# Flamingo block with cross-attention and an eight-expert FFN: first-layer weights loaded ahead of the slot reads, and the second early turn half a layer sooner

## The chip, the cores and the metric

The kernel runs on one core of one Trainium2 chip. The metric is device time in microseconds (us) of one execution, lower is better. The engines are PE (TensorE), DVE (VectorE), ACT (ScalarE), POOL (GpSimd) and SP (SyncE, which here only issues DMAs and waits).

## The reference

Four sequences of 512 tokens with 256 features. A 16-head cross-attention with mask and additive bias is followed by a feed-forward layer with 8 experts, of which each token uses the one with the highest gate value:

```python
x = x + tanh(g_xattn) * attention(layernorm(x), ctx, ctx, adj, mask)      # 4 x 512 x 256, 16 heads
h = layernorm(x).reshape(-1, 256)                                        # 2048 tokens
p = softmax(h @ gate_w.T); e = argmax(p)                                 # 8 experts
y = relu(h @ w1[e] + b1[e]) @ w2[e] + b2[e]                              # 256 -> 1024 -> 256
x = x + tanh(g_ffn) * (y * p[e])
```

## The kernel before, in words

**Attention.** A batch is one sequence. For each batch, 64 steps (`TILES`) each compute the scores of 128 queries against 512 keys for one head on PE (L931), take the row minimum and add the bias on DVE (L1551), shift on POOL (L672) or ACT (L1234), transpose on PE (L941), take the exponential on ACT (L1209), and every eighth step group is weighed with the values on PE (L953, `weigh`). Output projection, normalisation and routing of a batch are spread over the steps by tables (`USES`, `LAST_USES`). All engines run written-out programs and meet in semaphores only.

**Routing.** Each token gets a place in a table in DRAM, `slot_d`: routing goes in five rounds of four 128-token tiles, one round in each batch's steps and the last behind them, and for each tile POOL writes 128 entries of 8 bytes (token number and weight) by an indirect DMA (`to_slots`, L635). The table is later read back 128 entries at a time; such a group of 128 tokens of one expert is called a slot. There are 23 slots. The first five (`EARLY`) are full before the last round, whatever it brings, and are worked on beside the tail of the last batch; the other 18 (`LATE`) follow in a loop.

**One slot.** SP reads the slot's entries (`slots<-slot_d`) and the 1 MB first-layer weights of its expert (w1: 128 partitions of 8 KB). POOL gathers the 128 normalised rows from `xn_d` (L651 for the early ones, L732 later) and the 128 residual rows from `x1_d` (L658, L739). PE turns the rows (`early_turn`, L1019; `turn_rows`, L1095), ACT copies them to SBUF (`turned_rows`, L1272), PE computes the first layer in two halves of 16 matmuls (`early_hidden`, L1031; L1106), ACT applies the relu (`hidden`, L1278), PE computes the second layer (L1044; L1116), DVE adds bias and residual, and POOL scatters the rows to the output. The second-layer weights of all eight experts (w2, 1 MB each) stay in SBUF (`w2s`), which during attention holds the stacked queries and keys; the space of experts 4 and 6 is free after three quarters of the last batch's scores, that of 5 and 7 after all of them. No second layer starts before all eight have landed.

**SP's queue before,** from there on: w2 of experts 4 and 6 (after 48 of 64 score steps); w1 of early slot 0 when the early experts are known (`e_eid`); when the entries of the first four rounds have landed (`r_scat`), the five early slot reads; w1 of early slots 1 and 2; the attention output's rows to DRAM (`tail_pair`), and a wait until those have landed; w2 of experts 5 and 7; w1 of early slots 3 and 4. After the last routing: a wait for `r_eid` (experts of the late slots known) and `r_scat` (last entries written), the reads of late slots 0 and 1, their w1 loads, then a loop that reads each next slot and its weights when the buffers come free.

**POOL** waits for the five early slot reads (`early_index`) at step 59 of the last batch, in between two shifts that the attention steps need, then gathers the rows of early slot 0 and, three steps later, of early slot 1.

In the names of the trace, `w2s<-in_L_ffn_w` is a w2 load, and a load from `in_L_ffn_w` into `adjr`, `parts`, `xcin` or `pt` is a w1 load (their buffers are reused space). `parts<-xn_d,eidx` is the gather of an early slot's rows; `xT` from L1272 is the turned rows' copy, `adjm` the hidden layer's output.

Of the kernel before, what the change touches and what calls it, by code (L numbers as in the profile page):

```python
# [25 lines left out]
def build(nc, x, ctx_in, mask, g_xattn, g_ffn, adj, Wq, bq, Wk, bk, Wv, bv, Wo, bo,  # L26
          gate_w, w1, b1, w2, b2, out):
    B, S, E = x.shape
    X, _, DFF = w1.shape
    D = P // PAIRS  # L30
    H = E // D
# [21 lines left out]
    TILES = GROUPS * TPG  # L53
# [101 lines left out]
    with ExitStack() as st:  # L155
# [156 lines left out]
        def xg_bank(u):  # L312
            return bank[0][:, u * E:(u + 1) * E]

        def h_bank(u, c):
            return bank[1 + 2 * u + c // 4][:, (c % 4) * P:(c % 4 + 1) * P]
# [47 lines left out]
        def _(sp):  # L364
# [58 lines left out]
            def tail_pair(b, t, k, nxt):  # L423


                for u in range(2):
                    next_xres(b, nxt, k + u)
                for u in range(2):
                    rows_out(b, t, k + u)
                rows_free(b, k)  # L430
# [31 lines left out]
            def load_w2(e):  # L462
                sp.dma_start(w2s[:, e], w2[e].rearrange("(c p) f -> p c f", p=P)).then_inc(r_w2, 16)


            last = B - 1
# [9 lines left out]
            def early_w1(s):  # L476
                u = s % len(ew1)
                e = sp.value_load(eid[0:1, s:s + 1], min_val=0, max_val=X - 1)
                sp.dma_start(ew1[u], w1_v[ds(e, 1)].rearrange("x p k f -> p (x k) f")).then_inc(e_w1[u], 16)

            sp.wait_ge(s_stack, last * STACKED)
            sp.wait_ge(s_score, last * TILES + 6 * TILES // 8)
            for e in range(X // 2, X, 2):
                load_w2(e)
            sp.wait_ge(e_eid, 1)
            early_w1(0)
            sp.wait_ge(r_scat, B * (16 * QT))
            for s in range(EARLY):
                at = sp.value_load(base_i[0:1, s:s + 1], min_val=0, max_val=X * TOK)
                sp.dma_start(slots[:, s], slot_d[ds(at, P), :]).then_inc(e_slots, 16)  # L490
            sp.wait_ge(s_xT, B * 4)
            for s in range(1, 3):
                early_w1(s)
            tail_pair(last, last * QT, 2, last * QT + 2)
            sp.wait_ge(s_score, B * TILES)
            for e in range(X // 2 + 1, X, 2):
# [9 lines left out]
            def load_slots(j, v, after=None):  # L506


                at = sp.value_load(base_i[0:1, ds(j + EARLY, 1)], min_val=0, max_val=X * TOK)
                if after is not None:  # L510
                    sp.wait_ge(f_xt, after + EARLY)
                sp.dma_start(slots[:, ds(j + EARLY, 1), :].rearrange("p s a -> p (s a)"),
                             slot_d[ds(at, P), :]).then_inc(r_slots[v], 16)

            def load_w1(j, v, after=None):

                e = sp.value_load(eid[0:1, ds(j + EARLY, 1)], min_val=0, max_val=X - 1)
                if after is not None:
                    sp.wait_ge(f_h, FC * (after + EARLY))
                sp.dma_start(w1s[:, v], w1_v[ds(e, 1)].rearrange("x p k f -> p (x k) f")).then_inc(f_w1[v], 16)  # L520

            sp.wait_ge(r_eid, 1)
            sp.wait_ge(r_scat, (B + 1) * (16 * QT))
            for v in range(2):
                load_slots(v, v)
            for v in range(2):
                load_w1(v, v)
            with sp.Fori(0, LATE // 2 - 1) as i:
                for v in range(2):
                    load_slots(i * 2 + (v + 2), v, i * 2 + v + 1)  # L530
# [257 lines left out]
        def _(pe):  # L788
# [227 lines left out]
            def early_turn(s):  # L1016
                pe.wait_ge(e_row[s % EROWS], 16 * (s // EROWS + 1))
                for k in range(EC):
                    mm = pe.transpose(xg_bank(s % 2)[:, k * P:(k + 1) * P],  # L1019
                                      erow[s % EROWS][1][:, k * P:(k + 1) * P], ident[:])  # L1020
                mm.then_inc(f_xt, 1)

            def early_hidden(s, half):
                u = s % 2
                w = s % len(ew1)
                if half == 0:
                    pe.wait_ge(e_w1[w], 16 * (s // len(ew1) + 1))
                    pe.wait_ge(f_xgT, s + 1)
                for c in range(half * FC // 2, (half + 1) * FC // 2):
                    for k in range(EC):  # L1030
                        mm = pe.matmul(h_bank(u, c), ew1[w][:, k, c * P:(c + 1) * P], xgT[:, u, k],  # L1031
                                       start=k == 0, stop=k == EC - 1)
                    mm.then_inc(f_h, 1)
# [14 lines left out]
            def last_tail(what, k=0):  # L1048
                i = next(i for i, (n, w, a) in enumerate(TAIL_A) if w == what and (what == "gate" or a == k))
                tail_use(B, i + LAST_SHIFT, what, TAIL_A[i][2])  # L1050
# [9 lines left out]
            pe.wait_ge(s_osb, B * GROUPS + 2)  # L1060
            last_tail("heads", 0)
            last_tail("heads", 1)
            early_hidden(0, 1)
            early_turn(1)
            last_tail("turn", 0)
            last_tail("turn", 1)
            early_hidden(1, 0)
# [64 lines left out]
        def _(act):  # L1132
# [137 lines left out]
            def turned_rows(s, u):  # L1270
                act.wait_ge(f_xt, s + 1)
                act.activation(xgT[:, u], xg_bank(u).rearrange("p (k q) -> p k q", k=EC),  # L1272
                               ACT.Copy).then_inc(f_xgT, 1)

            def hidden(s, u, e, half):
                act.wait_ge(f_h, s * FC + (half + 1) * (FC // 2))
                for c in range(half * FC // 2, (half + 1) * FC // 2):
                    act.activation(hT[:, u, c], h_bank(u, c), ACT.Relu, bias=b1c[:, ds(e * FC + c, 1)]  # L1278
                                   ).then_inc(f_hT, 1)

            def expert_of(s):
                return act.value_load(eid[0:1, ds(s, 1)], min_val=0, max_val=X - 1)

            def last_tail(what, k):
                i = next(i for i, (n, w, a) in enumerate(TAIL_A) if w == what and a == k)
                tail_use(B, i + LAST_SHIFT, what, k)
# [7 lines left out]
            act.wait_ge(e_eid, 1)  # L1294
            e = expert_of(0)
            hidden(0, 0, e, 0)
            hidden(0, 0, e, 1)
            turned_rows(1, 1)
            last_tail("turn", 0)
            last_tail("turn", 1)  # L1300
            e = expert_of(1)
# [5 lines left out]
            e = expert_of(2)  # L1307
# [4 lines left out]
            for s in range(3, EARLY):  # L1312
                e = expert_of(s)
# [451 lines left out]
```

## Time and profile before

| | |
|---|---|
| time, median of 3 runs | 571.88 us (569.12 to 575.5) |
| the profiled execution's own time | 572.78 us |
| its span, first to last instruction | 570.8 us |
| PE busy | 532.1 us, 93% of the span |
| DVE, ACT, POOL busy | 298.7, 304.6, 304.2 us |
| mean granted TensorE clock | 0.996 |
| the chain that ended last | PE 51%, DMA 18%, issue 10%, DVE 7%, POOL 5% |

The profiled execution took 2.0 us more than its span, which is start and end outside the instructions. Times inside the trace are counted from the span's start. The attention ends at about 378 us and the late loop begins at about 431 us; the change touches what lies between 349 and 432 us. The profiled execution lies 0.9 us above the median of the three timed runs.

### The profile page before, as it was taken

What the parts mean: (1) busy time and instruction counts of PE and PEld (TensorE: products, weight loads), DVE (VectorE), ACT (ScalarE), POOL (GpSimd) and SP (SyncE); (2) the same over time, 40 slices, a digit from 0 to 9 for tenths busy, and PEclk for the clock granted to TensorE, in tenths of its full rate; (3) what the DMA queues carried; (4) which work ended last, traced back from release to release, by engine and by line L of the source; (5) the groups of instructions that cost most, each with busy time, mean ns of one, the idle gap of its engine ahead of it and who ended that gap; (6) DMA issues with size and microseconds to landing.
All of it is one profiled execution on the core that took longest, in us unless ns stands there. A gap on an engine that the chain in (4) does not pass through costs nothing.

```text
span 570.8 us, 13582 instructions
## 1 busy us (share of the span) xinstructions
PE 532.1 (93%) x4126; PEld 405.8 (71%) x4127; DVE 298.7 (52%) x908; ACT 304.6 (53%) x675; POOL 304.2 (53%) x461
## 2 busy tenths in 40 slices
PE   7999999989999989999999998879997899999996
PEld 5576666657566657666666765548897899999995
DVE  2676677875577876576876878813510111111111
ACT  4466676666677566678665676443232233333331
POOL 6345476765466665467573646451425445544441
PEclk9999999999999999999999999989999999999999
DMA  8633526301216410105510078778137656555650
GB/s 280 206 107 101 170 87 201 103 20 48 101 39 201 131 41 1 76 18 167 177 49 1 28 247 213 161 258 313 57 37 279 195 166 163 189 196 192 198 186 6
DMA packets 51392, 77.22 MB, mean 135 GB/s; under 512 B 9945, under 2 KB 34601, under 8 KB 51209
## 3 DMA queue, kind: packets, MB, share of 16 engines
q1 hardware_dynamic: 46600, 67.72, 37.2%
q0 software_dynamic: 4096, 8.29, 5.2%
q8 instruction: 29, 0.48, 0.4%
q10 hardware_dynamic: 640, 0.52, 0.3%
q14 instruction: 27, 0.21, 0.2%
HBM read 52.76 MB, written 7.89 MB: 106 GB/s over the span
## 4 chain that ended last, share of the span: by engine, by line
PE 51%; DMA 18%; issue 10%; DVE 7%; POOL 5%; ACT 4%; SPq 4%; POOLq 1%; DVEq 0%; ACTq 0%
PE bank L941 13%; DMA out_y<-cT,sidx 10%; PE bank L953 9%; PE bank L931 7%; PE bank L834 4%; DVE prob L1551 3%; DMA slot_d<-pair,posi 3%; SPq L345 3%; PE bank L1116 2%; PE bank L869 2%; PE bank L915 2%; PE bank L1031 2%; PE bank L1106 2%; ACT pt L1209 2%; POOL rows L739 2%
## 5 line engine op out<-in xcount | busy, mean ns | idle before, releaser
L1551 DVE CUSTOM_DVE_ANT_0 prob<-bank,adjm 128x512 f32<-128x512 f32 x256 | 172.5, 687 | 82.1 <-issue 50.1
L672 POOL TENSOR_SCALAR prob<-prob,negmax 128x512 f32<-128x512 f32 x192 | 133.2, 698 | 130.6 <-DVE negmax L1551 125.7
L1209 ACT ACTIVATE pt<-bank 128x512 f32<-128x512 f32 x256 | 150.3, 594 | 87.6 <-PE bank L941 83.3
L941 PE MATMUL bank<-ident,prob 128*128 128x128 f32 x1024 | 154.8, 274 | 4.6 <-POOL prob L672 2.3
L941 PEld LDWEIGHTS bank<-ident,prob 128*128 128x128 f32 x1024 | 124.2, 141 | 43.5 <-issue 14.7
L1278 ACT ACTIVATE adjm<-bank,colsm 128x128 f32<-128x128 f32 x184 | 52.6, 368 | 107.5 <-PE bank L1106 86.0
L931 PE MATMUL bank<-w2s 128*128 128x512 bf16 x256 | 97.5, 381 | 7.6 <-DVE negmax L1551 4.9
L953 PE MATMUL bank<-pt,vals 128*32 128x256 f32 x1024 | 69.1, 389 | 0.7 <-DVE vals L1365 0.5
L1727 DVE TENSOR_TENSOR cT<-bank,maski 128x256 f32<-128x256 f32 x18 | 7.6, 424 | 117.3 <-PE bank L1116 103.3
L1106 PEld LDWEIGHTS bank<-xT,pt 128*128 128x128 f32 x576 | 67.1, 192 | 1.8 <-ACT xT L1272 1.0
L1106 PE MATMUL bank<-xT,pt 128*128 128x128 f32 x576 | 67.3, 275 | 0.7 <-ACT xT L1272 0.7
L1116 PE MATMUL bank<-w2s,adjm 128*128 x288 | 65.4, 380 | 0.0
L1234 ACT ACTIVATE prob<-prob,negmax 128x512 f32<-128x512 f32 x64 | 45.9, 717 | 31.5 <-DVE negmax L1551 31.2
L1116 PEld LDWEIGHTS bank<-w2s,adjm 128*128 128x128 f32 x288 | 53.3, 190 | 6.5
L931 PEld LDWEIGHTS bank<-w2s 128*128 128x128 bf16 x256 | 25.7, 100 | 29.9 <-DVE negmax L1551 14.6
L953 PEld LDWEIGHTS bank<-pt,vals 128*32 128x32 f32 x1024 | 27.0, 109 | 23.0 <-issue 10.2
L635 POOL DMA_INDIRECT slot_d<-pair,posi x20 | 21.0, 1049 | 12.0 <-DVE posi L1474 5.1
L748 POOL DMA_INDIRECT out_y<-cT,sidx x18 | 18.1, 1007 | 15.0 <-DVE cT L1732 10.1
L732 POOL DMA_INDIRECT rows<-xn_d,gidx x18 | 18.0, 998 | 14.3 <-POOL gidx L730 14.3
L739 POOL DMA_INDIRECT rows<-x_d,xidx x18 | 17.4, 969 | 14.2 <-POOL xidx L737 14.2
L601 POOL TENSOR_TENSOR adjm<-adjr,maski 128x512 f32<-128x512 f32 x16 | 20.6, 1285 | 2.6 <-ACT maski L1198 2.4
L1551 DVE DVE_READ_ACCUMULATOR2_ANT negmax<- 128x1 f32 x256 | 20.9, 82 | 0.0
(192 smaller groups left out, 604.0 us busy)
## 6 DMA issues: line engine op xcount, KB each, us to landing
pt<-in_L_ffn_w SPq DMA_DIRECT2D x19, 1024.0 KB, 5.2
w2s<-parts SPq DMA_DIRECT2D x96, 128.0 KB
w2s<-in_L_ffn_w SPq DMA_DIRECT2D x8, 1024.0 KB, 9.9
maski<-in_mask_Bx1xSxS_ik SPq DMA_DIRECT2D x4, 1024.0 KB, 5.4
w2s<-parts SPq DMA_DIRECT2D x56, 64.0 KB, 2.1
xres<-in_x SPq DMA_DIRECT2D x18, 128.0 KB, 2.2
x_d<-rows SPq DMA_DIRECT2D x18, 128.0 KB, 1.7
xn_d<-rows SPq DMA_DIRECT2D x18, 128.0 KB, 2.5
```

The source lines that it names most:

```text
L672: po.tensor_scalar(prob[:, m], prob[:, m], -1.0, negmax[:, m:m + 1], ALU.mult, ALU.add).then_inc(s_shpool, 1)
L739: po.indirect_dma_start(rows[:, v, 0:E], None, x1_d, bass.IndirectOffsetOnAxis(ap=xidx[:, v:v + 1], axis=0)).then_inc(f_x1[v], 16)
L834: mm = pe.matmul(o[:], wT[:, w, k, m * P:(m + 1) * P], src[:, k], start=k == 0, stop=k == EC - 1)
L931: pe.matmul(sc_bank[m][:], q, k, start=True, stop=True).then_inc(s_score, 1)
L941: mm = pe.transpose(tr_bank[n % NTB][:, c * P:(c + 1) * P], prob[:, n % TILES % NB, c * P:(c + 1) * P], ident[:])
L953: mm = pe.matmul(pv_bank[32 * j:32 * j + 32, (g % 2) * HALF:(g % 2 + 1) * HALF], vals[:, c, hg * HG + j, :], pt[:, g % 2, c, j, :], start= ...
L1106: mm = pe.matmul(h_bank(u, c), w1s[:, v, k, c * P:(c + 1) * P], xgT[:, u, k], start=k == 0, stop=k == EC - 1)
L1116: mm = pe.matmul(y_bank(u), hT[:, u, c], w2s[:, ds(e, 1), c, :].rearrange("p x e -> p (x e)"), start=c == 0, stop=c == FC - 1)
L1209: act.activation(pt[:, g % 2, :, j, q2 * P:(q2 + 1) * P], tr_bank[c % NTB][:].rearrange("p (c q) -> p c q", c=QT), ACT.Exp).then_inc(s_cac ...
L1234: act.activation(prob[:, m], prob[:, m], ACT.Identity, scale=-1.0, bias=negmax[:, m:m + 1]).then_inc(s_shact, 1)
L1278: act.activation(hT[:, u, c], h_bank(u, c), ACT.Relu, bias=b1c[:, ds(e * FC + c, 1)]).then_inc(f_hT, 1)
L1551: ve.tensor_tensor_reduce(out=prob[:, m % NB], in0=sc_bank[m % NS][:], in1=adjm[:, qt], scale=-1.0, scalar=BIG, op0=ALU.add, op1=ALU.min, ...
```

## The change

Four edits. In the last batch SP issues w1 of early slots 0, 1 and 2 first, then reads the five slots, and only then loads w2 of experts 4 and 6. After the last routing, w1 of late slots 0 and 1 is loaded when the experts are known, before the wait for the table's last entries and before the two slot reads. On PE, `early_turn(1)` moves ahead of the second half of early slot 0's first layer, and on ACT `turned_rows(1, 1)` with it. Nothing is added or removed: each engine has as many instructions as before.

```diff
             sp.wait_ge(s_stack, last * STACKED)
-            sp.wait_ge(s_score, last * TILES + 6 * TILES // 8)
-            for e in range(X // 2, X, 2):
-                load_w2(e)
             sp.wait_ge(e_eid, 1)
-            early_w1(0)
+            sp.wait_ge(s_xT, B * 4)
+            for s in range(3):
+                early_w1(s)
             sp.wait_ge(r_scat, B * (16 * QT))
             for s in range(EARLY):
                 at = sp.value_load(base_i[0:1, s:s + 1], min_val=0, max_val=X * TOK)
                 sp.dma_start(slots[:, s], slot_d[ds(at, P), :]).then_inc(e_slots, 16)
-            sp.wait_ge(s_xT, B * 4)
-            for s in range(1, 3):
-                early_w1(s)
+            sp.wait_ge(s_score, last * TILES + 6 * TILES // 8)
+            for e in range(X // 2, X, 2):
+                load_w2(e)
             tail_pair(last, last * QT, 2, last * QT + 2)
...
             sp.wait_ge(r_eid, 1)
+            for v in range(2):
+                load_w1(v, v)
             sp.wait_ge(r_scat, (B + 1) * (16 * QT))
             for v in range(2):
                 load_slots(v, v)
-            for v in range(2):
-                load_w1(v, v)
...
+            early_turn(1)
             early_hidden(0, 1)
-            early_turn(1)
             last_tail("turn", 0)
...
             hidden(0, 0, e, 0)
+            turned_rows(1, 1)
             hidden(0, 0, e, 1)
-            turned_rows(1, 1)
```

SP in the last quarter of the last batch, before (L463 loads w2, L479 loads w1, L490 reads a slot; in brackets the semaphores that it waits for):

```order
L463 DMA w2s<-in_L_ffn_w 128x8x256 [waits score,stack]
L463 DMA w2s<-in_L_ffn_w 128x8x256
L478 TENSOR_LOAD eid [waits e_eid]
L478 ISA x2
L479 ISA
L479 DMA adjr<-in_L_ffn_w 128x2x1024
L489 TENSOR_LOAD base_i [waits r_scat]
L489 ISA x2
L490 ISA
L490 DMA slots<-slot_d 128x2
```

The same place now begins with three w1 loads; the five slot reads follow them.

```order
L478 TENSOR_LOAD eid [waits xT,e_eid,stack]
L478 ISA x2
L479 ISA
L479 DMA adjr<-in_L_ffn_w 128x2x1024
L478 TENSOR_LOAD eid
L478 ISA x2
L479 ISA
L479 DMA parts<-in_L_ffn_w 128x2x1024
```

Behind the last of the five slot reads SP now has the w2 pair, ahead of `tail_pair`:

```order
L489 DMA slots<-slot_d 128x2
L463 DMA w2s<-in_L_ffn_w 128x8x256 [waits score]
L463 DMA w2s<-in_L_ffn_w 128x8x256
L402 DMA xres<-in_x 128x256 [waits t_x1] x2
L407 DMA x_d<-rows 128x256 [waits t_row]
L408 DMA xn_d<-rows 128x256
```

The w2 loads have moved from the head of this stretch to behind the reads, and two w1 loads from behind the reads to ahead of them.

SP after the last routing, before (L512 reads a slot, L520 loads w1):

```order
L509 TENSOR_LOAD base_i [waits t_out0,t_x2T,t_out1,r_scat,r_eid]
L509 ISA x2
L512 ISA
L512 DMA slots<-slot_d 128x2
L509 TENSOR_LOAD base_i
```

And now, from the second of the two w1 loads (L519) to the first slot read; the wait for `r_eid` alone stands before the first of them:

```order
L516 TENSOR_LOAD eid
L516 ISA x2
L519 ISA
L519 DMA pt<-in_L_ffn_w 128x2x1024
L508 TENSOR_LOAD base_i [waits r_scat]
L508 ISA x2
L511 ISA
L511 DMA slots<-slot_d 128x2
```

The wait for `r_scat` stands behind the two w1 loads now.

ACT around early slot 0's hidden layer, before: the copy of early slot 1's turned rows (L1272) follows both halves (L1278).

```order
L1278 ISA
L1278 ACTIVATE adjm<-bank,colsm 128x128
L1272 ACTIVATE xT<-bank 128x2x128 [waits f_xt]
L1181 ACTIVATE atT<-bank 128x256 [waits m]
L1181 ACTIVATE atT<-bank 128x256 [waits t_atT,m]
```

Now it stands between the two halves:

```order
L1277 ISA
L1277 ACTIVATE adjm<-bank,colsm 128x128
L1271 ACTIVATE xT<-bank 128x2x128 [waits f_xt]
L1277 ISA [waits f_h]
L1277 ACTIVATE adjm<-bank,colsm 128x128
```

One copy has moved ahead of four relu instructions; PE's turn of the same rows has moved ahead of 16 matmuls in the same way.

## Rows read from the trace of the kernel before

**Rows 1.** Chain of waits, 320 to 381 us (start, length, what).

```profile
...
354.31 10.65 DMA slot_d<-pair,posi
...
370.19 1.70 DMA slots<-slot_d
...
373.12 7.55 DMA parts<-xn_d,eidx
...
```

**Rows 2.** Timeline of SP's DMA issues, 345 to 376 us.

```profile
...
349.57 1.12 SPq L463 DMA_DIRECT2D w2s<-in_L_ffn_w  x2
359.32 0.39 SPq L479 DMA_DIRECT2D adjr<-in_L_ffn_w  x1
365.70 4.84 SPq L490 DMA_DIRECT2D slots<-slot_d  x5
371.31 0.40 SPq L479 DMA_DIRECT2D parts<-in_L_ffn_w  x1
372.46 0.40 SPq L479 DMA_DIRECT2D xcin<-in_L_ffn_w  x1
...
```

**Rows 3.** Timeline of POOL, 370 to 380 us (in brackets: idle before, releaser).

```profile
...
372.05 0.19 POOL L645 COPY eidx<-slots 128x5 int32<-128x5 int32 x1 [1.78 <-DMA slots<-slot_d]
...
374.27 1.36 POOL L672 TENSOR_SCALAR prob<-prob,negmax 128x512 f32<-128x512 f32 x2
...
```

**Rows 4.** Timeline of PE, 373.5 to 392 us.

```profile
...
373.76 1.07 PE L953 MATMUL bank<-pt,vals 128*32 128x256 f32 x16
...
377.58 0.66 PE L941 MATMUL bank<-ident,prob 128*128 128x128 f32 x4 [0.50 <-POOL prob L672]
380.80 0.41 PE L1019 MATMUL bank<-ident,parts 128*128 128x128 f32 x2 [2.56 <-DMA parts<-xn_d,eidx]
381.14 2.75 PE L953 MATMUL bank<-pt,vals 128*32 128x256 f32 x32
383.81 2.86 PE L1031 MATMUL bank<-xT,adjr 128*128 128x128 f32 x16
...
391.02 2.02 PE L1031 MATMUL bank<-xT,parts 128*128 128x128 f32 x16 [1.04 <-ACT xT L1272]
...
```

**Rows 5.** Timeline of ACT, the last exponential of attention.

```profile
...
378.27 0.60 ACT L1209 ACTIVATE pt<-bank 128x512 f32<-128x512 f32 x1 [0.37 <-PE bank L941]
...
```

**Rows 6.** Busy us per engine in stretches, PEclk, DMA share (us), GB/s.

```profile
...
364.00:366.00 2.00, 1.68 (x12) 1.00 (x10) 1.97 (x5) 1.72 (x5) 1.18 (x3) 1.00 0.65 66
382.00:384.00 2.00, 2.00 (x21) 0.74 (x14) 0.00 (x0) 0.07 (x1) 0.43 (x1) 0.53 0.70 242
384.00:386.00 2.00, 2.00 (x12) 2.00 (x13) 0.00 (x0) 0.32 (x1) 0.00 (x0) 0.62 0.22 65
388.00:390.00 2.00, 1.99 (x18) 1.75 (x17) 0.68 (x2) 0.53 (x3) 0.00 (x0) 1.00 1.05 359
416.00:422.00 6.00, 6.00 (x41) 5.59 (x41) 1.16 (x3) 2.33 (x9) 0.00 (x0) 1.00 0.48 26
428.00:431.00 3.00, 0.23 (x3) 0.20 (x2) 0.91 (x2) 0.00 (x0) 2.21 (x4) 1.00 1.04 386
...
```

**Rows 7.** Gathers issued 373 to 376 us: count, median us to landing.

```profile
...
parts<-xn_d,eidx POOLq DMA_INDIRECT x2, 7.5
```

**Rows 8.** The same, issued 398 to 401 us.

```profile
...
parts<-xn_d,eidx POOLq DMA_INDIRECT x2, 3.7
```

**Rows 9.** Chain of waits, 380 to 570 us.

```profile
...
413.37 8.71 DMA slot_d<-pair,posi
...
```

**Rows 10.** Timeline of all engines, 413 to 433 us.

```profile
...
414.57 0.28 DVE L1718 TENSOR_SCALAR base_i<-bf,least 128x19 int32<-128x19 f32 x1
...
424.80 0.18 POOL L730 COPY gidx<-slots 128x1 int32<-128x1 int32 x1 [9.16 <-DMA slots<-slot_d]
...
425.81 0.99 POOL L732 DMA_INDIRECT rows<-xn_d,gidx  x1 [0.83 <-POOL gidx L730]
...
430.79 0.41 PE L1095 MATMUL bank<-ident,rows 128*128 128x128 f32 x2 [2.77 <-DMA rows<-xn_d,gidx]
...
```

## The prediction

> **What bounds the kernel now.** I read the chain of waits first, then the timelines of the engines around the places that the diff touches, then the DMA views there. PE is busy 93% of the span, but the chain leaves PE between 354 and 381 us. There it runs through the last table write of POOL, which needs 10.65 us to land, the five slot reads (1.70 us for the last), and the gather of early slot 0's rows, 7.55 us [rows 1]. PE meanwhile works off the attention and then stands for 2.56 us until the rows are there [rows 4]. A second, smaller stop is the 1.04 us before early slot 1's first layer: PE waits for ACT's copy of the turned rows, which queues behind slot 0's relus [rows 4]. The third place is the start of the late loop, where PE stands 2.77 us for gathered rows [rows 10]. The reader should see in each case which step lands last, because the change moves only steps of SP's queue and one turn.
>
> **The w2 pair leaves the table writes' time.** The two w2 loads are issued from 349.57 us, w1 of slot 0 at 359.32, and the table writes are in flight until 354.31 + 10.65 = 364.96 [rows 1, 2]. At the end of the kernel the same four writes run with next to nothing beside them (26 GB/s in all) and the last needs 8.71 us from its issue [rows 6, 9]. So without the pair the wait for `r_scat` should end 1.9 us sooner, at 363.0, as the near bound. The early writes are issued at wider distances, so that less is queued when the last one goes out; I take 360 to 361 us, an estimate, and keep 363 to 365 as the bad end.
>
> **Three w1 loads go ahead of the reads.** SP spends 1.15 us per w1 load (371.31 to 372.46) [rows 2]. Starting at 359.32 it is through with three at 362.8. The five reads are issued over 4.84 us [rows 2], the last at 367.4, and it lands 1.70 us later [rows 1] or when the 3 MB ahead of it are through. At the 359 GB/s of a stretch full of weight loads [rows 6] these 3.15 MB take 8.8 us, from 360 to about 368.8. So the table is read at 369 to 369.5, against 371.9 before. POOL, which stood 1.78 us for it [rows 3], no longer waits, and its shifts from 374.27 on come up to 1.78 us sooner. PE's last transposes follow such a shift after a wait of 0.50 us [rows 4], but PE has the 16 matmuls from 373.76 to 374.83 ahead of them; I count 0.9 us. That puts PE's end of the attention at 377.3 in place of 378.24.
>
> **The w2 pair comes behind the reads.** It is issued at about 367.9 and moves from 369. Behind it stand two loads and four stores of `tail_pair`, 0.79 MB, then POOL's gather, now issued at about 371.3. The pair and the rows are 2.9 MB, 8.0 us at 359 GB/s, so until 377; the gather lands at about 378. **Here I chose against an even share:** the gather issued at 373.12 with 2 MB of w1 just ahead took 7.5 us, the same gather later 3.7 [rows 2, 7, 8]. It behaved as if it queued behind what was issued first. The Trainium skill ("DMA: Bandwidth & Descriptors", Queues, rings and completion order) says that each DMA engine goes round its queues packet by packet, so a gather on POOL's queue would not wait out SP's loads, and the gain here would be the 3.1 us worked out below. In this trace the gather's 7.5 us speaks against it.
>
> **What PE gets of it.** Turn at 378.0, then the weighing at about 378.5; it began at 381.14 before [rows 4]. Its own inputs are no bar: the last exponential ends at 378.87 [rows 5], less the 0.9 us that moves with the shifts. That is **2.6 us**. Were the gather there at 377.3 the weighing would begin at 378.0, and the gain be 3.1; should the writes still land at 363 to 365, the reads, the pair and the gather all move back two to three us, and no more than 0.5 to 1 us is left.
>
> **The clock.** After the stop of 2.56 us the granted clock is 0.53 and 0.62 in the next two stretches of 2 us [rows 6], which is 1.2 GHz for most of them. 32 weighing matmuls take 2.75 us there, where 16 took 1.07, and 16 of the first layer take 2.86, where 2.02 is usual [rows 4]: (2.75 - 2.14) + (2.86 - 2.02) = 1.45 us. With a stop of 0.7 us instead I expect the clock to stay at 2.4 GHz, **1.5 us**; zero is the other end, since in the stop of 2.77 us at 428 us [rows 10] the granted clock stayed at 1.00 [rows 6], so the link is not a firm one.
>
> **The turn sooner.** PE's turn of slot 1 stands ahead of 16 matmuls, and ACT copies its rows ahead of four relus. The rows are needed at about 383.5 then, after the weighing and half a first layer; their gather goes out some 3 us behind slot 0's, near 374, and has 9 us. PE goes from the attention's turns straight into slot 1's first layer: the 1.04 us of [rows 4] goes, and ACT's later copies for the output projection are covered by these 16 matmuls (2.02 us). **1.0 us.**
>
> **The w2 pair of experts 5 and 7, and the second layer.** That pair waits for `tail_pair` to land, which is not later than before, since less is queued ahead of it. The first second layer is far behind; I put this at nothing. If it were late, PE would wait for it whole.
>
> **The late loop's start.** The experts are known at 414.85 us [rows 10], so the two w1 loads go out at about 415.5 and 416.7, while the table writes are in flight until 413.37 + 8.71 = 422.08 [rows 9]. That gives and takes. The gather issued at 425.81 has landed by 430.7, 4.9 us later [rows 10], with a w1 load issued just ahead of it; without one it should take 3.7 us [rows 8], which gives up to 1.1. But while table writes are in flight other transfers crawl: 66 GB/s in a stretch before 366 with w1 of slot 0 outstanding, 26 GB/s at 416 to 422 with a gather outstanding [rows 6]. At 66 GB/s only 0.4 MB of the 2.1 MB are through by 422, and the rest needs 4.7 us at 359 GB/s, to 426.8. The slot reads stand behind it in SP's queue; the first had landed by 424.80 before [rows 10], and would now land 2.0 us later: 1.0 us lost. At full rate the pair would be through in time and the 1.1 stay whole. I take a loss of **0.7 us**, near the slow end, because both rows with table writes in flight are slow ones. What the loads do to the writes themselves is a rival.
>
> **The sum.** 2.6 + 1.5 + 1.0 - 0.7 = 4.4 us. The profiled execution's 572.78 us would be 568.4, and the median of 571.88 becomes **567.5 us**, 0.8% less. About 1% is what a measurement of this kernel can tell from no change.
>
> **Rivals.**
> (a) Everything comes out at its good end: the gather is not held by the w2 pair, and the late w1 pair is through before the reads: 3.1 + 1.5 + 1.0 + 1.1 = 6.7, so 565.2 us. For it: DMA is all but idle at 416 to 422, and the gathers of [rows 8] needed 3.7 us only. Against it: the 7.5 us of [rows 7], and the 66 GB/s. Chance 0.27. The skill's rule on the queues, above, would make the first part of it true.
> (b) The early table writes do not land sooner, because three w1 loads press on them in place of two w2 loads. Then the chain through table, reads and gather keeps its length: 0.8 + 0 + 1.0 - 0.7 = 1.1, so 570.8 us. For it: 10.65 us against 8.71 with and without loads, so loads do press. Against it: the w1 loads start 5 us after the last write is issued. Chance 0.2.
> (c) Slower than before: the two late w1 loads lengthen the last table writes, on which the late slot reads, and PE behind them, wait. If the writes wait out the pair as the gather of 7.5 us waited out 2 MB, they land 2.1 MB / 359 GB/s = 5.8 us later; the reads then have nothing ahead of them and the gather gives its 1.1. With the early part as in (b), 0.8 + 1.0 - 5.8 + 1.1 = -2.9, so 574.8 us. It decides once the writes land later by more than the early gains and 1.1 us: by 6.2 us if the early gains come whole, by 2.9 if they are those of (b). For it: 10.65 us with loads beside against 8.71 without. Against it: that is 1.9 us, not 5.8. Chance 0.06.
> (d) The change does not do what it says: the stop before the first turn stays because something else is last, such as the row gather behind `tail_pair`'s stores. That is the time of (b), and is in its chance.
>
> **How the numbers follow.** Forecast 0.47, (a) 0.27, (b) and (d) 0.2, (c) 0.06. Faster by over 1% means under 566.2 us: (a), and a little of the forecast's spread, 0.31. Slower by over 1% is over 577.6, beyond (c) as worked out; 0.04 is for the spread of the runs around it (569.12 to 575.5 before). The rest is 0.65. The range goes from 564.4, a little below (a), to 571.4, just beyond (b).
>
> **What would show it.** In the changed kernel's timelines: w2 of experts 4 and 6 issued at 367 to 369; no idle time of POOL before L645; the first early turn with at most 1 us of idle before it, at 377 to 379; no clock under 1.00 at 380 to 386; no wait for ACT before slot 1's first layer. In the late part, seen from the last table write's issue, its landing after 9 to 11 us and PE's first late turn after about 18 us, where it was 17.4. I am wrong if the table writes before 365 still take over 10 us from the last issue, if the gather still takes over 7 us and PE's stop stays, or if the last writes take 12 us and more.

## The result, and the profile after

The changed kernel needs 575.39 us (median of 20 runs, 572.03 to 578.27), the kernel before 571.92 (20 runs, 568.31 to 578.33). The ratio is 1.0063, 95% interval 1.0038 to 1.0087: 3.6 us slower, 2.2 to 5.0, where 4.4 us faster was forecast. The profiled execution after took 573.35 us (span 571.5, mean granted clock 0.989), the one before 572.78. Its own time hides most of the loss, so the places have to be read one by one.

SP's queue after, the place of [rows 2]:

```profile
...
359.40 0.39 SPq L479 DMA_DIRECT2D adjr<-in_L_ffn_w  x1
360.59 0.38 SPq L479 DMA_DIRECT2D parts<-in_L_ffn_w  x1
361.73 0.38 SPq L479 DMA_DIRECT2D xcin<-in_L_ffn_w  x1
362.89 4.85 SPq L489 DMA_DIRECT2D slots<-slot_d  x5
367.78 1.06 SPq L463 DMA_DIRECT2D w2s<-in_L_ffn_w  x2
...
380.33 1.01 SPq L463 DMA_DIRECT2D w2s<-in_L_ffn_w  x2
...
412.05 1.15 SPq L519 DMA_DIRECT2D pt<-in_L_ffn_w  x2
...
```

POOL and PE after, from the index copy to early slot 1's first layer, the places of [rows 3, 4]:

```profile
...
371.38 0.19 POOL L644 COPY eidx<-slots 128x5 int32<-128x5 int32 x1 [1.07 <-DMA slots<-slot_d]
...
```

```profile
...
378.81 0.41 PE L1018 MATMUL bank<-ident,parts 128*128 128x128 f32 x2 [1.12 <-DMA parts<-xn_d,eidx]
379.15 1.93 PE L952 MATMUL bank<-pt,vals 128*32 128x256 f32 x32
381.02 2.05 PE L1030 MATMUL bank<-xT,adjr 128*128 128x128 f32 x16
...
386.57 1.95 PE L1030 MATMUL bank<-xT,parts 128*128 128x128 f32 x16
...
```

The edits did what they say. PE's stop before the first early turn is 1.12 us in place of 2.56, the weighing begins at 379.15 in place of 381.14 and takes 1.93 us in place of 2.75, and the wait for ACT's copy is gone (386.57 has none). So far the profile is nearly the one that was forecast: the stop was to be at most 1 us, the weighing to begin 2.6 us sooner (it is 2.0), and POOL, which was no longer to wait for the slot reads, still stands 1.07 us for them. The chain of waits shows the other half, beside [rows 1, 9]:

```profile
...
367.39 3.83 DMA slots<-slot_d
...
372.44 5.91 DMA parts<-xn_d,eidx
...
408.84 9.59 DMA slot_d<-pair,posi
...
419.16 6.79 DMA slots<-slot_d
...
```

The last table write goes out at 408.84, 4.5 us sooner than 413.37. But the slot reads, issued when it has landed, need 6.79 us. In the kernel before, the chain has 1.72 us for them:

```profile
...
422.92 1.72 DMA slots<-slot_d
...
```

Timelines of POOL and PE after, beside [rows 10]:

```profile
...
426.11 0.18 POOL L729 COPY gidx<-slots 128x1 int32<-128x1 int32 x1 [14.99 <-DMA slots<-slot_d]
427.12 0.99 POOL L731 DMA_INDIRECT rows<-xn_d,gidx  x1 [0.83 <-POOL gidx L729]
...
```

```profile
...
409.06 3.73 PE L1030 MATMUL bank<-xT,pt 128*128 128x128 f32 x32
...
430.08 0.66 PE L1094 MATMUL bank<-ident,rows 128*128 128x128 f32 x2 [6.38 <-DMA rows<-xn_d,gidx]
431.29 6.28 PE L1105 MATMUL bank<-xT,pt 128*128 128x128 f32 x32 [0.54 <-ACT xT L1271]
437.41 0.38 PE L1094 MATMUL bank<-ident,rows 128*128 128x128 f32 x2
...
```

PE stands for 6.38 us where it stood for 2.77, and its first late layer takes 6.28 us where 32 such matmuls took 3.73 at 409.06. The stretches after tell both (busy us of each engine, granted clock, DMA share, GB/s; beside [rows 6]):

```profile
...
360.00:362.00 2.00, 1.69 (x11) 1.45 (x12) 1.72 (x8) 1.25 (x3) 1.18 (x2) 1.00 0.62 80
362.00:364.00 2.00, 2.00 (x26) 1.18 (x24) 1.82 (x6) 0.88 (x2) 0.20 (x1) 1.00 1.02 406
364.00:366.00 2.00, 1.71 (x12) 1.03 (x10) 1.96 (x5) 1.72 (x5) 1.15 (x3) 1.00 1.03 422
380.00:382.00 2.00, 2.00 (x30) 1.38 (x21) 0.00 (x0) 0.00 (x0) 1.45 (x2) 1.00 0.52 123
...
412.00:414.00 2.00, 2.00 (x15) 1.71 (x14) 0.00 (x0) 1.65 (x7) 0.00 (x0) 1.00 0.77 27
414.00:416.00 2.00, 2.00 (x11) 1.77 (x10) 0.00 (x0) 0.80 (x4) 0.00 (x0) 1.00 0.66 64
416.00:418.00 2.00, 2.00 (x18) 1.92 (x17) 0.91 (x2) 0.00 (x0) 0.00 (x0) 1.00 1.04 63
418.00:420.00 2.00, 2.00 (x21) 2.00 (x20) 0.00 (x0) 1.14 (x4) 0.00 (x0) 1.00 0.61 162
420.00:422.00 2.00, 2.00 (x12) 1.79 (x11) 0.00 (x0) 1.14 (x4) 0.00 (x0) 1.00 1.05 420
422.00:424.00 2.00, 1.71 (x8) 1.15 (x7) 0.15 (x1) 0.00 (x0) 0.00 (x0) 1.00 0.92 359
424.00:426.00 2.00, 0.00 (x0) 0.00 (x0) 0.76 (x2) 0.00 (x0) 0.00 (x0) 1.00 0.09 17
426.00:428.00 2.00, 0.00 (x0) 0.00 (x0) 0.00 (x0) 0.00 (x0) 1.06 (x2) 0.55 0.00 0
432.00:434.00 2.00, 2.00 (x11) 2.00 (x11) 0.00 (x0) 0.00 (x0) 1.19 (x3) 0.50 0.28 68
...
```

The granted clock is 1.00 behind the early stop (380 to 382) and 0.50, the lower level, behind the late one. The two w1 loads were issued from 412.05. While the table writes are in flight, to 418.43, the DMA engines show shares of 0.77, 0.66 and 1.04 and still move only 27 to 64 GB/s: 0.31 MB in six us. Then come 162, 420 and 359 GB/s, 1.88 MB, and at 424 the traffic is over. The read lands 1.95 us after that.

### The profile page after: what moved, and what is told of

Read it like the earlier page. It is cut to its first block, busy times and chain, and to the rows that moved or that the text cites. A ratio compares the mean times of both kernels' runs of the same rounds, so it can differ in the third digit from the quotient of the medians.

```text
span 571.5 us, 13581 instructions
## 1 busy us (share of the span) xinstructions
PE 532.6 (93%) x4126; PEld 407.1 (71%) x4127; DVE 298.9 (52%) x908; ACT 304.6 (53%) x675; POOL 304.0 (53%) x461
## 4 chain that ended last, share of the span: by engine, by line
PE 47%; DMA 18%; issue 11%; DVE 8%; POOL 5%; SPq 4%; ACT 4%; POOLq 1%; another core or an unknown queue 1%; DVEq 0%; ACTq 0%
PE bank L940 13%; DMA out_y<-cT,sidx 10%; PE bank L952 9%; PE bank L930 7%; DVE prob L1550 4%; PE bank L833 4%; SPq L345 3%; PE bank L868 2%; PE bank L914 2%; ACT pt L1208 2%; DMA slots<-slot_d 2%; PE bank L1115 2%; POOL rows L738 2%; DMA slot_d<-pair,posi 2%; PE bank L1030 2%
## 5 line engine op out<-in xcount | busy, mean ns | idle before, releaser
L1105 PEld LDWEIGHTS bank<-xT,pt 128*128 128x128 f32 x576 | 69.5, 198 | 1.8 <-ACT xT L1271 0.9
L1105 PE MATMUL bank<-xT,pt 128*128 128x128 f32 x576 | 69.8, 281 | 0.5 <-ACT xT L1271 0.5
L738 POOL DMA_INDIRECT rows<-x_d,xidx x18 | 17.4, 969 | 14.2 <-POOL xidx L736 13.4
```

The source lines that it names most:

```text
L738: po.indirect_dma_start(rows[:, v, 0:E], None, x1_d, bass.IndirectOffsetOnAxis(ap=xidx[:, v:v + 1], axis=0)).then_inc(f_x1[v], 16)
L1105: mm = pe.matmul(h_bank(u, c), w1s[:, v, k, c * P:(c + 1) * P], xgT[:, u, k], start=k == 0, stop=k == EC - 1)
```

## The experiments

Each ratio is to the kernel before, measured beside it. "Late pair ahead" is the edit behind the last routing; "early edits" are the other three. What was read from each profiled execution stands together here, in us. The fourth column is from the issue of the last table write to its landing, the fifth from that issue to the first late turn, the sixth the rest of the span from that issue. The last says behind which of PE's two stops (before the first early turn, before the first late turn) the granted clock fell to 0.50.

| kernel | first early turn | last table write issued | it lands after | late turn after | rest of span | half clock behind the stops |
|---|---|---|---|---|---|---|
| before | 380.80 | 413.37 | 8.71 | 17.42 | 157.4 | early |
| before_2 | 380.30 | 412.68 | 9.97 | 18.86 | 158.1 | both |
| before_3 | 380.74 | 413.31 | 9.11 | 18.06 | 157.4 | both |
| before_busy | 382.19 | 413.19 | 10.14 | 18.94 | 158.2 | none |
| turn_only | 380.90 | 412.89 | 9.10 | 17.94 | 160.4 | both |
| sp_early_only | 379.90 | 412.42 | 8.95 | 19.00 | 161.9 | both |
| early_only | 379.26 | 409.35 | 9.86 | 18.76 | 158.1 | late |
| early_only_2 | 381.77 | 411.45 | 9.59 | 18.35 | 159.4 | late |
| x_later | 380.31 | 410.00 | 8.97 | 17.72 | 161.4 | late |
| late_busy | 379.95 | 411.26 | 9.52 | 18.27 | 157.8 | early |
| busy_both | 380.13 | 409.84 | 9.47 | 18.30 | 161.0 | none |
| late_only | 381.36 | 413.91 | 9.96 | 21.93 | 164.8 | both |
| after | 378.81 | 408.84 | 9.59 | 21.24 | 162.7 | late |
| after_2 | 380.64 | 410.31 | 10.08 | 22.01 | 164.5 | late |
| pool_reads | 380.53 | 410.29 | 10.43 | 22.00 | 163.9 | late |
| after_busy | 380.79 | 412.10 | 10.55 | 22.40 | 164.1 | both |
| one_w1 | 381.97 | 413.20 | 9.46 | 18.85 | 163.2 | both |

**early_only**: all edits but the late one. The late part is as before:

```diff
             sp.wait_ge(r_eid, 1)
-            for v in range(2):
-                load_w1(v, v)
             sp.wait_ge(r_scat, (B + 1) * (16 * QT))
             for v in range(2):
                 load_slots(v, v)
+            for v in range(2):
+                load_w1(v, v)
```

> All edits but the late one: after the last routing SP again waits for the table's last entries, reads late slots 0 and 1, and then loads their w1. Theory Q (the loss is made in the late part: the slot reads stand behind 2 MB of w1 in SP's queue, and PE's longer stop brings the slow clock): the early part gains what the trace of the changed kernel shows at its last routing, 4.5 us, so about 567.5 us, ratio to before 0.990 to 0.994. Theory W (the w1 loads lengthen the last table writes, and that is the whole loss): the same 567.5, last write 8.7 us from its issue to landing. Theory E (the early part itself loses in most executions and the one trace is not typical): 573 us or more.

Measured: 0.9981, interval 0.9951 to 1.0011 (572.96 us). Its chain of waits:

```profile
...
372.88 6.17 DMA parts<-xn_d,eidx
...
409.35 9.86 DMA slot_d<-pair,posi
...
420.04 1.73 DMA slots<-slot_d
...
422.94 4.83 DMA rows<-xn_d,gidx
...
```

The read is back at 1.73 us. So the loss is in the late edit, and the early ones gain 1.1 us or nothing that can be told. The first two theories expected about 567.5 us here, the 4.5 us of the one trace of after; that did not come.

**late_only**: the kernel before with the late edit alone.

```diff
             sp.wait_ge(r_eid, 1)
+            for v in range(2):
+                load_w1(v, v)
             sp.wait_ge(r_scat, (B + 1) * (16 * QT))
             for v in range(2):
                 load_slots(v, v)
-            for v in range(2):
-                load_w1(v, v)
```

> Only the late edit: w1 of late slots 0 and 1 ahead of the wait for the table's last entries and of the two slot reads. Theory Q: the reads land about 6.8 us after their issue where it was 1.7, PE's first late turn begins 21 us after the last table write's issue (17.4 before), and the clock is slow for part of the next 10 us: 4 to 8 us slower than before, 576 to 580. Theory W: the last write needs 12 us and more, the reads still 1.7. Theory E: no difference from before.

Measured: 1.0083, 1.005 to 1.0117 (579.69 us), 4.7 us slower. The two halves add up to the whole: 0.9981 and 1.0083 against 1.0063. Its chain:

```profile
...
413.91 9.96 DMA slot_d<-pair,posi
...
424.60 7.11 DMA slots<-slot_d
...
```

The write lands after 9.96 us, within the 8.71 to 10.14 of the kernels without the late edit; the read takes 7.11. It is mainly the reads that wait, not the writes.

**after_busy**: the changed kernel with PE's late stop filled, by the kernel's own `keep_busy` (matmuls of ones that nothing reads).

```diff
             pe.wait_ge(r_w2, 16 * X)
+            keep_busy(55, bank[7])
             turn_rows(0, 0)
```

> The changed kernel with 55 matmuls of ones into a free bank between the last early second layer and the first late turn, some 6 us of PE work while it would stand; they compute nothing that is used. Theory Q with the clock as part of it: no slow clock between 420 and 440 us, 3 us or more faster than the changed kernel, 571 to 573 us. If the clock has no part in the loss: the same as the changed kernel, 575.

Measured: 1.0068, 1.0038 to 1.0098 (578.72 us). PE's idle time before the late turn falls to 1.48 us, the turn comes no sooner (22.40 us after the write's issue), and the half clock is still there, shorter: under 1.00 at 434 to 440, where in after it was from 426 to 438. Shortening it gains nothing that can be told (1.0068 against 1.0063); since the clock did fall, the run does not show what none of it would give. Two things say that it is not the cause: the late turn is late before the slow stretch costs anything, and before_2 and before_3 have the half clock behind the late stop too and end 158.1 and 157.4 us after the last table write's issue, where before ends after 157.4 without it.

**pool_reads**: the changed kernel, in which POOL issues the first two late slot reads on its own queue.

```diff
             for v in range(2):
                 load_w1(v, v)
-            sp.wait_ge(r_scat, (B + 1) * (16 * QT))
-            for v in range(2):
-                load_slots(v, v)
...
+            for v in range(2):
+                at = po.value_load(base_i[0:1, v + EARLY:v + EARLY + 1], min_val=0, max_val=X * TOK)
+                po.dma_start(slots[:, v + EARLY], slot_d[ds(at, P), :]).then_inc(r_first[v], 16)
```

> The changed kernel, with the reads of late slots 0 and 1 issued by POOL on its own queue (after the same waits) in place of SP. Theory Q in the form that only SP's own queue holds the reads back: they land within 3 us of their issue although the w1 pair is still loading, PE's first late turn begins 18 us after the last table write's issue, and the time is 568 to 571. If the DMA engines work off all queues in the order of issue: the reads land after 5 to 7 us as in the changed kernel, and the time is 575.

Measured: 1.0073, 1.0042 to 1.0105 (577.98 us). The chain's row of the read, and the stretches from there:

```profile
...
422.57 5.63 DMA slots<-slot_d
...
```

```profile
...
422.00:424.00 2.00, 2.00 (x11) 1.74 (x10) 0.00 (x0) 1.03 (x4) 0.85 (x2) 1.00 1.02 414
424.00:426.00 2.00, 1.21 (x6) 0.73 (x4) 0.61 (x2) 0.00 (x0) 0.30 (x1) 1.00 1.00 391
426.00:428.00 2.00, 0.00 (x0) 0.00 (x0) 0.30 (x1) 0.00 (x0) 0.00 (x0) 0.90 0.24 93
...
```

Another queue gives no way past: the read takes 5.63 us, and lands 2 us after full traffic ended at about 426.2. POOL issues it 1.85 us behind the landing of the writes, SP did after 0.73, and so it lands 17.9 us after the last write's issue, as in after_2. POOL's own gather ahead of it, issued at 411.57, had landed 9.3 us later, before the read went out, so it did not hold the read. That SP's own queue orders the read behind the loads falls as the cause; the bytes issued first were served first, or nearly so, across the queues. No run has a read on POOL's queue with nothing ahead, so what this queue adds of itself is not known.

**one_w1**: only the first late w1 load ahead of the reads.

```diff
-            for v in range(2):
-                load_w1(v, v)
+            load_w1(0, 0)
             sp.wait_ge(r_scat, (B + 1) * (16 * QT))
             for v in range(2):
                 load_slots(v, v)
+            load_w1(1, 1)
```

> The changed kernel with one late w1 load ahead of the wait for the table and of the reads, the second behind them. Theory Q (reads stand behind the bytes issued before them): some 0.3 MB pass while the table is written, 0.7 MB are left, so the reads land 3.5 to 4.5 us after their issue (6.8 with two loads, 1.7 with none), and the time lies about half way between the changed kernel and the kernel with the early edits alone: 2 us under the changed one. Theory W (the loads lengthen the table writes, whatever their number): no better than the changed kernel.

Measured: 1.0037, 1.001 to 1.0063 (574.78 us). Half the bytes ahead, about half the length:

```profile
...
413.20 9.46 DMA slot_d<-pair,posi
...
423.72 4.16 DMA slots<-slot_d
...
```

1.73, 4.16 and 6.8 to 7.1 us with none, one and two loads of 1 MB ahead: 2.4 to 2.9 us for each, about what 1.05 MB take at 359 to 420 GB/s. But in this trace the first late turn comes 18.85 us after the write's issue, within the 17.4 to 19.0 of the kernels with no load ahead: the gather behind the read, with no load just ahead of it, takes back what the read lost. The time is 2.1 us longer all the same, and the trace has 4.2 us of PE's waits for gathered rows after 440 us, where the others have 0 to 3.1. So the dose shows the read's length, and not that the whole of the time follows from it.

**turn_only** and **sp_early_only** halve the early edits: the second early turn (on PE and ACT) alone, and SP's new order up to `tail_pair` alone.

```diff
+            early_turn(1)
             early_hidden(0, 1)
-            early_turn(1)
```

> Of the changed kernel only the early turn of slot 1 and its copy half a layer sooner. PE's wait of 1.0 us before slot 1's first layer is gone; the last table write is issued 1.0 us sooner. 1.0 us faster if the late part hands it on; the same if the table writes or the clock take it back.

> Of the changed kernel only SP's early order (three w1 loads, slot reads, then w2 of experts 4 and 6); the turn and the late order as before. By the first traces (last routing 1.3 to 4.5 us sooner with the early order and the turn together) I expect the last table write of POOL issued 1 to 3 us sooner than before, and 1 to 3 us of time, if the late part gives nothing back; no gain if it does.

Measured: 0.998, 0.9947 to 1.0013, and 0.9996, 0.9969 to 1.0023. In turn_only PE no longer waits for the turned rows' copy. In sp_early_only the first early turn comes 0.4 to 0.9 us sooner than in the three traces of before. Their sum is about that of early_only; neither can be told from nothing.

**x_later**: early_only with the gather that follows the last table writes on POOL (the residual rows of early slot 4) moved behind the first two late gathers.

```diff
             for t in range(QT):
                 to_slots(t)
-            early_x(EROWS + 1)
...
             for v in range(2):
                 gather_normed(v, 0, v)
+            early_x(EROWS + 1)
```

> The kernel with the early edits alone, and POOL's gather of early slot 4's residual rows moved from right behind the last table writes to behind the two gathers of late rows. It asks what holds the table writes up, which need 8.7 to 9.9 us from the last issue with no load beside them but this gather. If the gather presses on them: 7 to 8 us, and up to 2 us less time than with the early edits alone. If they are slow by themselves: unchanged, and the later gather may cost some tenths of a us because an early output waits for it.

Measured: 0.9983, 0.995 to 1.0016 (570.6 us). The writes land after 8.97 us, in the lower part of what is seen with the gather; no effect on the time can be told from early_only's.

**busy_both**, **before_busy** and **late_busy** fill PE's stops: the early edits with both filled, the kernel before with both filled, the early edits with the late one filled.

```diff
             pe.wait_ge(e_eid, 1)
+            keep_busy(12, bank[2])
             early_turn(0)
...
             pe.wait_ge(r_w2, 16 * X)
+            keep_busy(30, bank[7])
             turn_rows(0, 0)
```

> The kernel with the early edits alone, and matmuls of ones into free banks where PE stands: 12 (1.3 us) before the first early turn, 30 (3.2 us) before the first late turn; they compute nothing that is used. The traces so far have a stretch of slow clock behind one or both stops in every execution. If the clock is what takes the early gain back: no or less slow clock behind both, and 2 to 4 us less than before (ratio 0.993 to 0.997), 1 to 3 us less than with the early edits alone. If the clock falls all the same or is not the cause: as with the early edits alone, 0.998, or some tenths of a us more.

> The kernel before with 12 matmuls of ones ahead of the first early turn and 30 ahead of the first late turn, whose results nothing reads; no load is moved. If what made the kernel with the early edits and these matmuls 0.5% faster is only the clock, this one gains the same, 0.995 to 0.997, with the granted clock at 1.00 behind both stops; if it needs the earlier table writes as well (last one issued near 409.5 us in place of 413), this one lies at 0.998 to 1.000 and its last table write is issued at 412 or later.

> The early edits alone, with the 30 matmuls ahead of the first late turn and none at the early stop. If the slow clock at the late stop is what gives back the two to three us by which the early edits bring the last table write forward, this lies where the kernel with both fillings was, 0.994 to 0.997; if the late filling does nothing, it lies where the early edits alone were, 0.998, with later pauses of the loop taking what the clock gives.

Measured: 0.9954 (0.9923 to 0.9985, 571.72 us), 0.9968 (0.9938 to 0.9999, 573.48 us, its before 575.33) and 0.9965 (0.9934 to 0.9997, 571.48 us, the same before). Stretches of before_busy behind both stops, beside [rows 6]:

```profile
...
382.00:384.00 2.00, 1.81 (x30) 1.12 (x34) 0.00 (x0) 0.38 (x1) 1.70 (x2) 1.00 1.09 403
384.00:386.00 2.00, 2.00 (x26) 1.59 (x17) 0.00 (x0) 0.39 (x1) 0.06 (x1) 1.00 0.41 137
432.00:434.00 2.00, 1.23 (x9) 1.00 (x10) 0.00 (x0) 0.38 (x1) 1.21 (x3) 1.00 1.01 412
434.00:436.00 2.00, 2.00 (x21) 2.00 (x20) 0.00 (x0) 0.61 (x3) 1.39 (x3) 1.00 0.65 189
...
```

The clock holds at 1.00 behind both. All three are faster than before, busy_both by 0.46%, and that version beats both kernels. The filling alone gives 0.3%, the early edits alone 0.2% (not told from nothing), both 0.5%: the figures add, but the intervals overlap and do not tell the three apart.

**before_2**, **before_3**, **early_only_2** and **after_2** are one more profiled execution each of kernels that ran already.

> The kernel before once more, one look, since one trace of it stands for 20 runs that spread over 10 us. In its first trace the clock was slow behind the early stop (382 us) and not behind the late one. If that was typical: the same again, late turn 17.4 us after the last table write's issue and 140 us from there to the end. If it was a lucky execution: slow clock at the late stop too, and 142 to 143 us to the end.

> The kernel before a third time, the same question: is a slow clock behind the late stop, and how long are the steps from the last table write to the late turn (17.4) and from there to the end (140.0).

> The kernel with the early edits alone a second time, one look. Last table write's issue at 409.4 us if no slow clock follows the early stop, near 412 if one does; late turn 18 to 19 us later.

> The changed kernel once more, for a second trace. If the late loop's start is the cause, the first slot read again lands 6.5 to 7.2 us after its issue, and the first late turn comes 21 to 22.5 us after the last table write's issue; if the profiled execution was an odd one, these are nearer to the 1.7 and 18 us of the kernel before.

Their times were 572.66, 572.64, 572.72 and 576.67 us. after_2 repeats the read's length:

```profile
...
421.12 7.07 DMA slots<-slot_d
...
```

They show what one trace cannot: the half clock is behind the early stop in all traces with before's SP order and no filling there (five of five), and behind the late stop in two of before's three. The 1.00 of [rows 6] at 428 to 431, behind a stop of 2.77 us, was one execution's.

## Why the prediction was wrong

**The failed step is the late loop's start.** The term was a loss of 0.7 us; late_only gives 4.7 (2.9 to 6.7), and so does the changed kernel's ratio against early_only's. In the traces the first late turn comes 21.2 to 22.4 us after the last table write's issue with two w1 loads ahead (mean of five 21.9), and 17.4 to 19.0 without (mean of eleven 18.3): 3.6 us, where 0.7 was forecast. (The working gave 2.0 - 1.1 = 0.9; it was written as 1.0 and taken as 0.7, "near the slow end", without a row.) Step by step, counted from that issue in the changed kernel's trace:
- The pair was to be through after 13.4 us (426.8 against 413.37). It was through after some 15.2 (424 against 408.84). The loads went out 3.2 us after the write's issue, not 2.1. The crawl was in the sum, at 0.4 MB; it moved 0.3 MB, the write landed 0.9 us later, and the full rate came up only about a us behind the landing (162 GB/s at 418 to 420).
- The read was taken to land together with the pair. Its own 1.7 us (the last early read of [rows 1]) come on top: it landed 1.95 us after the traffic ended, 17.1 us after the write's issue, not 13.4. This is a little over half of the 3.7 us, and it needed no new price: the row was there, and I counted a transfer behind a load as one that ends with the load.
- The gather gained more than the 1.1 us of the forecast: PE turns 2.96 us after it is issued at 427.12, where it was 4.98 [rows 10]. That gives back 0.9 of the 3.7.

So the mechanism (reads queued behind w1, w1 crawling beside the writes) was right, but for the words "in SP's queue", which pool_reads takes out; the size at the turn was wrong by a factor of five. What is left of the 4.7 us, about 1 us, lies behind the late turn, where the rest of the span differs by more than the turn does; it isn't traced to one place.

**The w2 pair out of the writes' time: right in the writes, wrong in what follows.** The early entries had landed by 360.1 in the changed kernel, 359.7 to 363.5 in all traces with the new SP order, against 363.6 to 366.5 with the old one: the 360 to 361 of the estimate is the better end of that (means 361.6 and 365.1). But the reads landed at 371.2, where 369 to 369.5 was forecast. The w1 loads issued from 359.40 moved 80 GB/s until 362 and 406 to 422 after, so that 3.1 MB ended at about 369.5, and the read's own time came on top, again left out. That is the same mistake as in the late part, at the first place where I made it. In the other traces it is worse: POOL's gather of slot 0's rows went out at 373.4 in the mean of the eleven, at 372.9 in the five with the old order and no filling. The 3.5 us gained at the writes are gone by then.

**What PE gets of it: 2.6 us forecast, 0.5 measured.** The first early turn stands at 380.4 in the mean of the eleven traces with SP's new order, and at 380.8 in the five with the old one and no filling. In the trace of after the weighing began 2.0 us sooner; that trace is the best of the eleven, and the others are up to 3.2 us behind it. The 0.5 us are left of the gather, which went out 0.5 us later in the mean but took 6.8 us in place of 7.8. The stop, forecast at 0.7 us, went from 2.6 to 1.8 in the mean of the traces without filling.

**The gather behind the w2 pair** landed later than it would on a free way: 5.91 us in after, 6.94 and 7.33 in after_2 and one_w1, against 3.7 [rows 8]. I had chosen against an even share between the queues. That holds here, and pool_reads shows the same with the late read on a queue that had nothing else left in it. By the Trainium skill ("DMA: Bandwidth & Descriptors", Queues, rings and completion order) each DMA engine goes round its queues packet by packet, so that a read on another queue should pass the loads; the 5.63 us speak against it, as the 7.5 us of [rows 7] did. Rival (a), whose first part needed that rule, is out.

**The clock: 1.5 us forecast.** With the early edits the clock stayed at 2.4 GHz behind the early stop in six of the nine traces with no filling there, and not in three. The six stops before it were 1.12 to 1.96 us long, the three 1.90 to 2.34; with SP's old order the five were 1.99 to 3.29, and it fell behind each. Where it stayed, the last table write went out at 408.84 to 411.45; where it fell, at 411.26 to 413.20. Counted from the first early turn, it goes out after 29.7 to 30.1 us where the clock stayed, and after 31.2 to 31.3 where it fell: 1.5 us in the mean. So the term had the right size, and comes about two times in three. A stop of 1.96 us kept the clock and one of 1.90 did not, so the stop's length alone does not settle it.

**The turn sooner: 1.0 us forecast.** The wait is gone in every trace that has the edit, and turn_only's 0.998 is 1.1 us, with an interval that takes in zero. From the first early turn to the last table write, busy_both needs 29.7 us and before_busy 31.0, both at full clock, which is 1.3 (they differ in SP's order too); turn_only needs 32.0 against 32.4 to 32.6 in the three traces of before, about 0.5.

**The sum of the early terms** was 5.1 us. At the last table write the ten traces with all early edits stand at 410.7 in the mean, the five of the old order (turn_only apart) at 413.3: 2.6 us. That is about the 0.5 at the first early turn, 1.0 of the clock (two thirds of 1.5) and 1.0 to 1.3 of the sooner second turn; of the missing 2.5, some 2.1 are what the reads took back. In time early_only gives 1.1 (-0.6 to 2.8). Between the two lie PE's waits for `rows<-xn_d,gidx` after 440 us: none in the trace of early_only, 3.1 us in that of x_later. Whether the early edits cause them or the executions differ is open.

**The rivals.** (a) read the DMA as "all but idle" at 416 to 422; by bytes it is (26 GB/s), by the share of 0.48 in the same row it is not. (b) had the early part nearer, at 1.8 us against the 1.1 measured, by another way: the writes did land sooner, and the way through table and reads kept its length because the reads took longer. (c) had the sign and nearly the size, 574.8 us, but that is luck, since the mechanism was another. The writes with the pair beside them landed after 9.6 to 10.6 us (mean of five 10.1), without it after 8.7 to 10.1 (mean of eleven 9.4): 0.7 us, where 5.8 was its price. Slower by this way, the reads waiting out the whole pair and the writes little, was no rival of mine. It should have been: the case was worked out as a term of the sum and given no far end.

## What to carry to other kernels

In these runs a short transfer issued behind big loads cost the rest of those loads and its own latency besides, on either queue. So moving loads ahead "while the queues are idle" pays only if their bytes are through before the short transfer is issued, and bytes issued beside many 8-byte writes were not. Work out that end with the rate of the stretch in which the loads would move, and give it a far bound. A short DMA on a critical chain goes ahead of the loads, and where a stop of PE can't be removed, filling it may be worth as much as shortening it (0.3% and 0.2% here, not told apart).

## What the hardware showed that was not expected

- Four writes of 128 entries of 8 bytes, the last of which lands 8.7 to 10.6 us after its issue, leave other traffic little: with two loads of 1 MB outstanding, 27 to 64 GB/s passed in all until they landed (after), and the loads moved behind them. It isn't that the writes fill the engines all this time: in the trace of before, with no load, the DMA share was 1.24 at 416 to 418 and 0.12 and 0.07 in the four us up to the landing. What holds the loads is not shown.
- A read of 1 KB issued on POOL's queue took 5.63 us while another engine's loads of 2 MB, issued 9 us before it, were still being moved; on SP's queue the same read took 6.8 to 7.1 us behind them and 1.7 us with nothing ahead.
- The kernel before kept the full clock behind a late stop of 2.77 us in one execution and fell to half behind 3.41 and 4.20 us in two others; with PE filled up to the last 0.4 to 1.0 us it stayed at 1.00 in the traces of before_busy and busy_both. In after_busy, with 1.48 us left, it fell all the same.
